# A fused Perceiver layer on one core: new prologue order and stage table, and the FFN's last product as two reduced-precision products

## The reference

```
x = x + xattn(layernorm(x), ctx, ctx)    # Q,K,V = proj(+bias); 16 heads of 16; softmax; @ Wh.T + bh
x = x + attn(layernorm(x))               # causal linear attention: exp features of normalised q, k
x = x + ffn(layernorm(x)), where
  gate = x @ (w_gate/127).T ; up = x @ (w_up/127).T        # 768 hidden, integer weights -127..127
  h    = silu(gate) * up
  out  = h @ (w_down/127).T                                # "down": 256x768 times 768x256 per batch
```

## Time and profile before

| | |
|---|---|
| median of 3 runs (lowest, highest) | 905.61 us (902.4, 907.89) |
| the profiled execution's own time | 904.62 us |
| its span | 902.9 us |
| TensorE matmul busy | 838.8 us, 93% |
| VectorE busy | 424.6 us, 47% |
| ScalarE busy | 531.7 us, 59% |
| mean granted TensorE clock | 0.992 |

### The profile page before, as it was taken

The page is one execution under the profiler, slowest core; times in us unless marked ns, Lnnn a source line. Parts: engine busy times, 40 slices in busy tenths (PEclk is TensorE's granted clock), DMA queues, the critical chain, the costliest instruction groups (busy, mean ns, idle before and its releaser), DMA issues.

```text
span 902.9 us, 20688 instructions
## 1 busy us (share of the span) xinstructions
PE 838.8 (93%) x8883; PEld 578.2 (64%) x8883; DVE 424.6 (47%) x752; ACT 531.7 (59%) x578; POOL 47.8 (5%) x76
## 2 busy tenths in 40 slices
PE   6699999999999999999999999999899999988876
PEld 5566666656566666766656667766566666657655
DVE  6533235454644446534654446444654444213753
ACT  2177887767476666656557666666557666750101
POOL 1033000000000000000000000000000000000100
PEclk9899999999999999999999999999999999999989
DMA  6777664466333433246433332355433322201000
GB/s 174 233 216 225 214 205 166 141 213 189 114 142 141 141 141 117 100 159 176 142 140 142 141 114 88 128 187 139 166 140 141 119 111 77 71 23 26 1 1 15
DMA packets 58737, 120.08 MB, mean 133 GB/s; under 512 B 21521, under 2 KB 29713, under 8 KB 55121
## 3 DMA queue, kind: packets, MB, share of 16 engines
q1 hardware_dynamic: 56848, 114.31, 37.4%
q0 software_dynamic: 1792, 4.40, 1.7%
HBM read 78.84 MB, written 37.75 MB: 129 GB/s over the span
## 4 chain that ended last, share of the span: by engine, by line
PE 72%; DVE 12%; issue 6%; DMA 3%; ACT 3%; DVEq 2%; POOL 1%; SPq 0%; POOLq 0%; ACTq 0%
PE ps_o L752 22%; PE ps_s L764 16%; PE ps_pa L557 9%; PE ps_pa L596 9%; PE ps_pa L722 2%; ACT probs L1036 2%; PE ps_pa L697 2%; DMA oscr<-y 2%; PE ps_pa L709 1%; PE ps_pa L688 1%; PE ps_pa L674 1%; DVE kparts L1075 1%; DMA y<-oscr 1%; DVE feat L1276 1%; DVE ctx_lo L1061 1%
## 5 line engine op out<-in xcount | busy, mean ns | idle before, releaser
L1036 ACT ACTIVATE probs<-ps_s 128x1024 f32<-128x1024 f32 x512 | 496.2, 1023 | 250.6 <-PE ps_s L764 243.7
L752 PE MATMUL ps_o<-probs,values 128*17 128x256 f32 x4096 | 252.9, 381 | 0.0
L764 PEld LDWEIGHTS ps_s<-qstack,kstack 64*128 64x128 f32 x2048 | 138.7, 185 | 105.3 <-ACT probs L1036 54.4
L764 PE MATMUL ps_s<-qstack,kstack 64*128 64x256 f32 x2048 | 193.3, 305 | 9.6 <-ACT probs L1036 7.5
L752 PEld LDWEIGHTS ps_o<-probs,values 128*17 128x17 f32 x4096 | 103.3, 97 | 96.9 <-issue 7.9
L1073 DVE TENSOR_SCALAR kparts<-ps_pa,b_heads 128x512 fp32r<-128x512 f32 x64 | 48.0, 750 | 105.0 <-PE ps_pa L557 105.0
L1090 DVE TENSOR_TENSOR values<-ps_pa,bv_pair 128x512 f32<-128x512 f32 x64 | 44.2, 690 | 105.1 <-PE ps_pa L596 104.9
L596 PE MATMUL ps_pa<-wv_hi,ctx_hi 128*128 128x256 f32 x256 | 77.6, 303 | 2.1 <-DVE wv_lo L1061 1.6
L596 PE MATMUL ps_pa<-wv_lo,ctx_hi 128*128 128x256 f32 x256 | 72.1, 282 | 0.0
L596 PE MATMUL ps_pa<-wv_hi,ctx_lo 128*128 128x256 f32 x256 | 71.9, 281 | 0.0
L557 PE MATMUL ps_pa<-ctx_hi,wk_hi 128*128 128x512 f32 x128 | 58.0, 453 | 4.3 <-DVE kparts L1075 2.2
(11 more groups left out here) (238 smaller groups left out, 797.5 us busy)
## 6 DMA issues: line engine op xcount, KB each, us to landing
kstack<-kscr SPq DMA_DIRECT2D x96, 512.0 KB, 5.2
kscr<-kparts SPq DMA_DIRECT2D x64, 512.0 KB, 2.7
ctx_raw<-ctxT SPq DMA_DIRECT2D x32, 512.0 KB, 6.7
qstack<-qscr SPq DMA_DIRECT2D x12, 256.0 KB, 3.9
qscr<-qparts SPq DMA_DIRECT2D x4, 512.0 KB, 3.2
xh<-x SPq DMA_DIRECT2D x4, 256.0 KB, 5.9
kstack<-kstack SPq DMA_DIRECT2D x2, 512.0 KB, 6.4
qstack<-ksample SPq DMA_DIRECT2D x4, 256.0 KB, 3.8
```

Of the source, the lines that this page charges most:

```text
L752: last = mm(ps_o[32 * j:32 * j + DH + 1, g * S:(g + 1) * S], values[par][:, i, head_of_step(g, j), :], prob[:, j * S:(j + 1) * S], start=b ...
L764: last = mm(ps_s[s % 2][:, j * S:(j + 1) * S], kstack[par][rows, u, i * P:(i + 1) * P], queries[rows, u, :], start=True, stop=True)
L1036: nc.scalar.activation(probs[n % AHEAD][:, :], ps_s[n % 2][:, :], ACT.Exp, scale=float(DH) ** -0.5).then_inc(fast["exp_done"], 1)
```

## The change

1. Prologue. TensorE's first matmul no longer waits for the value bias. The weights `wq` are turned by ACT and not by VectorE, and are loaded ahead of the value bias, as `wv` is. `split_ctx(0)` stands ahead of the bias copy. Head stages go round four half banks of `ps_s`. The sampled maximum is worked out directly behind `q`; the values and the keys of chunk 1 come after it: values pair 0 ahead of the first score, pair 1 and both key units of chunk 1 in slots 0, 1 and 4 of chunk 0, whose own value slots move to 5 and 8. SP issues the shift ahead of the load of context chunk 2.
2. Tables. `AT` and `HEAD_AT` have new steps (the FFN stages and `down` earlier, the head stages earlier, `ln1T` to `norm1` later). `kbd` is cut into `kbd0` and `kbd1`. SP writes a batch's queries ahead of a key half in chunk 6, and stacks and shifts them in chunk 7 behind a wait for the previous tail's `down`.
3. The down product. `wd_sb` becomes fp32r (integers up to 127, exact in it). `gate{k}` on VectorE makes `hid` and then cuts it into a high and a low part, four blocks' parts in the idle query stack, two in `x_parts` (so gates 4 and 5 wait for `gu5`). `down_part` is then two fp32r matmuls where one fp32 matmul was. The integer weights come into `qk` and `y` in two DMAs and are cast from there.

```diff
 VALUE_SLOTS = {3: 0, 5: 1}
 KEY_SLOTS = {9: 0, 13: 1}
+FIRST_KEYS = {1: 0, 4: 1}
+FIRST_VALUES = {5: 0, 8: 1}
+HEAD = ["ln0", "ln0T", "q", "kbd0", "max0", "max1", "kbd1", "max2", "max3", "maxT"]
+HEAD_FIRST = ["ln0", "ln0T", "q", "kbd0", "kbd1", "max0", "max1", "max2", "max3", "maxT"]
-AT = {"o": 1, "oT0": 3, "oT1": 4, "yT": 12, "wh": 13, "ln1T": 17, "qk0": 19, "ss0": 19, "qk1": 21, "ss1": 21, "v": 24,
-      "norm0": 24, "norm1": 25, "qkT0": 25, "qkT1": 28,
+AT = {"o": 1, "oT0": 3, "oT1": 4, "yT": 12, "wh": 13, "ln1T": 19, "qk0": 20, "ss0": 20, "qk1": 22, "ss1": 22, "v": 24,
+      "norm0": 26, "qkT0": 26, "norm1": 27, "qkT1": 28,
...
-      "A4": 64, "A5": 70, "pv2": 72, "A6": 74, "A7": 78, "pv3": 82, "o2T0": 84, "o2T1": 85, "y2T": 88, "wout": 89,
-      "ln2T": 94, "gu0": 96, "gate0": 98, "gu1": 99, "gate1": 100, "gu2": 101, "gate2": 104, "gu3": 105, "gate3": 108,
-      "gu4": 109, "gate4": 112, "gu5": 115, "gate5": 116, "down": 124}
+      "A4": 64, "A5": 70, "pv2": 72, "A6": 74, "A7": 78, "pv3": 80, "o2T0": 84, "o2T1": 86, "y2T": 88, "wout": 90,
+      "ln2T": 94, "gu0": 96, "gate0": 98, "gu1": 100, "gate1": 101, "gu2": 102, "gate2": 103, "gu3": 104, "gate3": 105,
+      "gu4": 106, "gu5": 110, "gate4": 110, "gate5": 111, "down": 112}
-HEAD_AT = {"ln0": 86, "ln0T": 104, "q": 108, "kbd": 110, "max0": 112, "max1": 116, "max2": 117, "max3": 120,
-           "maxT": 121}
+HEAD_AT = {"ln0": 86, "ln0T": 92, "q": 99, "kbd0": 106, "max0": 108, "kbd1": 110, "max1": 114, "max2": 115,
+           "max3": 116, "maxT": 118}
...
-         **{f"max{n}": "kbd" for n in range(4)}}
+         **{f"max{n}": f"kbd{n // 2}" for n in range(4)}}
...
+        wd_int = [qk[:, :, :].rearrange("p t c -> p (t c)").bitcast(INT32).rearrange("p (k n) -> p k n", n=D),
+                  y[:, :, :].bitcast(INT32)]
         x_parts = [sb("x_hi", [P, CI, S], FP32R)[:, :, :], sb("x_lo", [P, CI, S], FP32R)[:, :, :]]
+        def hid_part(of, k, part):
+
+            n = 2 * k + part
+            return qstacks[of][:, n, :] if n < HALF else x_parts[(n - HALF) // CI][:, n % CI, :]
...
+            if alone == "head":
+                k = c.bank(clock, name) % BANKS_HEAD
+                return ps_s[k // 2][:, k % 2 * 512:(k % 2 + 1) * 512]
...
+        def keys_bank(q, j):
+
+            return ps_a if (q, j) in ((0, 1), (1, 0), (1, 1), (2, 0)) else ps_p
+
+        def parts_of(c, clock):
+
+            return 0 if c is general else clock[1] % 2
...
+            sp.dma_start(wq_rows.rearrange("p (i n) -> p i n", i=CI), wr(wqT)).then_inc(wq_in, 16)
+            sp.dma_start(wstage[:, CI * D:2 * CI * D].rearrange("p (i n) -> p i n", i=CI), wr(wvT)).then_inc(wv_in, 16)
             for t in range(2):
                 sp.dma_start(bv_pair[:, t * H:(t + 1) * H, :].rearrange("p h d -> p (h d)"),
-                             bv.partition_broadcast(P)).then_inc(b_in, 16)
-            sp.dma_start(wq_rows.rearrange("p (i n) -> p i n", i=CI), wr(wqT)).then_inc(wq_in, 16)
-            sp.dma_start(wstage[:, CI * D:2 * CI * D].rearrange("p (i n) -> p i n", i=CI), wr(wvT)).then_inc(wv_in, 16)
+                             bv.partition_broadcast(P)).then_inc(bv_in, 16)
...
             stack_queries(fast, 0, qstacks[0])
+            shift_queries(fast, head_of(0), qstacks[0])
+            load_ctx(fast, NCH, 2)
             sp.wait_ge(hot_in, 16)
             sp.dma_start(kstack[1][SLOTS:P:APART, :, :].bitcast(FP32), kstack[0][SLOTS:P:APART, :, :].bitcast(FP32)
                          ).then_inc(hot_in, 16)
-            load_ctx(fast, NCH, 2)
-            shift_queries(fast, head_of(0), qstacks[0])
             write_keys(fast, 1, 1)
...
+                    if b + 1 < B and p == HEAD_AT["q"] // STEPS:
+                        write_queries(fast, head_of(b + 1))
+                    if b + 1 < B and p == HEAD_AT["maxT"] // STEPS:
+                        if b:
+                            sp.wait_ge(fast["product"], fast.at("product", tail_of(b - 1), "down"))
+                        stack_queries(fast, b + 1, qstacks[(b + 1) % 2])
+                        shift_queries(fast, head_of(b + 1), qstacks[(b + 1) % 2])
                     if q + 2 < B * NCH:
                         write_key_half(fast, q + 2, p % 2, 0)
-                    if b + 1 < B and p == HEAD_AT["q"] // STEPS:
-                        write_queries(fast, head_of(b + 1))
-                        stack_queries(fast, b + 1, qstacks[(b + 1) % 2])
-                    if b + 1 < B and p == HEAD_AT["maxT"] // STEPS:
-                        shift_queries(fast, head_of(b + 1), qstacks[(b + 1) % 2])
                     if q + 2 < B * NCH:
                         write_key_half(fast, q + 2, p % 2, 1)
                     if b and p == AT["down"] // STEPS:
...
-                if j:
+                if q == 1:
+                    pe.wait_ge(fast["k_out"], 2 + j)
+                elif q == 2:
+                    pe.wait_ge(*((fast["v_ready"], q * PAIRS) if j else (fast["k_out"], q * 2)))
+                elif q and j:
                     pe.wait_ge(fast["k_out"], q * 2 + 1)
...
-            def down_part(c, k, bank, clock=None):
-
-                if clock is not None:
-                    pe.wait_ge(c["operand"], c.at("operand", clock, f"gate{k}"))
+            def down_part(c, k, bank, clock):
+
+                pe.wait_ge(c["operand"], c.at("operand", clock, f"gate{k}"))
                 for t in range(ST):
-
-                    last = mm(bank[:, t * D:(t + 1) * D], hid[:, k, t * P:(t + 1) * P], wd_sb[:, k, :],
-                              start=k + t == 0, stop=k == HB - 1, skip_group_check=True)
+                    for part in range(2):
+
+                        last = mm(bank[:, t * D:(t + 1) * D], hid_part(parts_of(c, clock), k, part)[:, t * P:(t + 1) * P],
+                                  wd_sb[:, k, :], start=k + t + part == 0, stop=k + part == HB, skip_group_check=True)
                 return last
...
-                if s in VALUE_SLOTS and q + 1 < B * NCH:
-                    project_values(q + 1, VALUE_SLOTS[s])
+                value_slots = VALUE_SLOTS if q else FIRST_VALUES
+                if q == 0 and s == 0:
+                    project_values(0, 1)
+                if q == 0 and s in FIRST_KEYS:
+                    project_keys(1, FIRST_KEYS[s])
+                if s in value_slots and q + 1 < B * NCH:
+                    project_values(q + 1, value_slots[s])
...
-            pe.wait_ge(b_in, 64)
+            pe.wait_ge(b_in, 32)
             pe.wait_ge(setup_dve, 2)
-            mm(ps_a[:, 0:2 * CI], ident_heads, b_rows[:, :], start=True, stop=True).then_inc(b_turned, 1)
-            project_keys(0, 0)
-            products(fast, ["ln0T"], head_of(0))
-            project_keys(0, 1)
+            mm(ps_s[1][:, 512:512 + 2 * CI], ident_heads, b_rows[:, :], start=True, stop=True).then_inc(b_turned, 1)
+            warm(ps_s[1], 5)
+            for j in range(CI):
+                project_keys(0, j)
+            products(fast, ["ln0T"], head_of(0), "head")
+            pe.wait_ge(wq_turned, 1)
+            products(fast, ["q"], head_of(0), "head")
+            warm(ps_p, 10)
+            products(fast, ["max0", "max1", "max2", "max3", "maxT"], head_of(0), "head")
             pe.wait_ge(setup_dve, 3)
-            products(fast, ["q"], head_of(0))
-            warm(ps_s[1], 7)
-            pe.wait_ge(setup_dve, 4)
-            for pair in range(PAIRS):
-                project_values(0, pair)
-                products(fast, [f"max{2 * pair}", f"max{2 * pair + 1}"], head_of(0))
-            project_keys(1, 0)
-            products(fast, ["maxT"], head_of(0))
-            project_keys(1, 1)
-            warm(ps_s[1], 12)
+            project_values(0, 0)
+            warm(ps_a, 3)
...
-            pool.dma_start(wd_sb[:, :, :].bitcast(INT32), wr(wdT)).then_inc(i_in, 16)
+            for k, part in zip((0, HB - CI), wd_int):
+                n = part.shape[1]
+                pool.dma_start(part, wr(wdT)[:, k:k + n, :]).then_inc(i_in, 16)
...
+            act.wait_ge(wq_in, 16)
+            nc.scalar.activation(by_heads(wq_sb), by_dims(wq_rows), ACT.Copy).then_inc(wq_turned, 1)
...
+                    if heads and n == 0:
                         dve.wait_ge(c["q_shift"], heads * 16)
-                    for j in range(CI):
-                        last = v.tensor_tensor(ksample[:, j, :, :],
-                                               kparts[:, 0, j, 0:SAMPLE].bitcast(FP32).unsqueeze(1).to_broadcast([P, H // 2, SAMPLE]),
-                                               head_mask[:, :].unsqueeze(2).to_broadcast([P, H // 2, SAMPLE]), ALU.mult)
+                    last = v.tensor_tensor(ksample[:, n, :, :],
+                                           kparts[:, 0, n, 0:SAMPLE].bitcast(FP32).unsqueeze(1).to_broadcast([P, H // 2, SAMPLE]),
+                                           head_mask[:, :].unsqueeze(2).to_broadcast([P, H // 2, SAMPLE]), ALU.mult)
...
```

(56 more changed lines are left out.)

47 lines of the change are left out of this document (23 added, 24 removed).

## The result

The changed kernel takes 911.5 us (median of 7 runs, 907.85 to 917.49), the kernel before, on the same chip, 905.5 (7 runs, 902.4 to 911.35). The ratio is 1.007, 95% interval 1.0042 to 1.0098: slower, by more than the 0.5% of a no-change. The forecast was 902.5, range 894.5 to 908, with 0.07 on slower. The profiled execution after is the fastest of its seven: own time 907.85, span 906.0. Its span is 3.1 us longer than that of before; the medians lie 6 apart.

What follows compares the result with a forecast made beforehand. TensorE was taken to bound the loop, with chains of engines in the prologue and last tail. The terms summed to -3.1 us, 904.62 to 901.5; with the median 1.0 higher, 902.5, range 894.5 to 908.

Steps and rivals of the forecast that it cites:

- First score: Prologue: the first score comes at 32.5 instead of 41.66, -9.2 us.
- Low clock behind the first score: Start of chunk 0: low clock lasts until 36, so 3.5 us behind the first score lose half, +1.5 us.
- Rival B: Chunk 0's first quads: TensorE stays at 1.2 GHz, deciding from a low clock until 42; up to 910 us, chance 0.12.
- the three units and batch 0's waits: Three units moved into chunk 0 cost +4.8 us; shorter waits at batch 1's first score and `max0` save 2.1.
- Added waits (a) to (d): In the loop, in order: `qkT0` 2.5, paired products 0.32, `down` 1.65, `max1` 0.9; +5.5, +1.3, +3.3, +1.8 us.
- 2.0 at `gu4`: Batch 3's last two chunks: 2.0 us idle at `gu3` and `gu4`, without a unit between, until ACT passes an exp.
- Rival A: Loop: the added waits at `qkT0`, `down` and `max1`, 10.6 us, don't come; 892 us, chance 0.32.
- Last two chunks of batch 3: From 763.5, the last value product ends at 810.4 instead of 811.1, -0.7 us.
- Down product: Batches 1 and 2: 24 fp32r matmuls take 2.85 us instead of 5.37, saving 2.5 each, -5.1 us.
- Rival C: Down product: weight loads don't overlap matmuls, so its 5.1 us saving is gone; 907.6 us, chance 0.02.
- Last tail: Serial end behind the loop: longer gates and `gu5` ahead of gates 4 and 5 put output at 900.75, +2.9 us.
- the signs that I had named for a wrong prediction: No waits at `qkT0` and `down`, or chunk 0 longer than 24 us by a stall before chunk 1's first score.

Runs made afterwards that it cites:

- the wait filled: The changed kernel with nine dummy matmuls issued on TensorE in the wait of `qkT0`, its late place kept: 907.6 us, ratio 1.0025 to the kernel before.
- the three groups: The follow-up kernels' runs, each group on one chip beside the kernel before, which took 905.1 to 906.0 us in them; the changed kernel did not run again.

## Why the prediction was wrong

Step by step, measured in the profiled executions, in which the change was forecast at -3.1 and came out at +3.1 of span:

- **First score** -9.2: came at 29.30, not 32.5, so -12.4. This term was mis-sized by the landing of the first context chunk. The earlier trace rows has three loads with 3.8, 4.2 and 6.8; I took the longest for the first. It was there by 5.5, and the cut ended at 7.5 for 10.1. This error went in the change's favour and hid a part of the others.
- **Low clock behind the first score** +1.5: the clock was 0.50 until 30.6, 1.3 us past the first score, and most of that lies before a wait for the exp. About half a microsecond. But this is one draw. In two other profiles with the same prologue (the wait filled, fp32 down in the changed kernel) it was low until 38.2 and 38.4, and `yT` of batch 1 came 2.2 and 2.8 us later. Rival B's 42 was not reached, a part of it was. With the three units and batch 0's waits the prologue and batch 0 were forecast at -5.0 and gave -8.9 at `yT` of batch 1.
- **Added waits (a) to (d)**: right in place and size (2.46 for 2.5, 0.29 to 0.34 for 0.32, 1.65 for 1.65, 0.78 for 0.9; 1.74 for 2.0 at `gu4` of batch 3). Rival A had no part in it.
- **What was missing in them**: the low clock. This is the step that failed. I priced an idle stretch of TensorE at its own length. In the terms of the prediction, (a), (c) and the 2.0 at `gu4` are waits without a term for what comes behind them. I had looked for low clock only in the prologue, because the loop of before runs at full clock with single waits of up to 1.76 (at `yT` of batch 2), and took that for a rule. Four falls in the profiled loop cost 1.7 each, 6.7 together.
- **`ln0T`** at step 92: its product waits 1.03 and 1.05 for the layernorm behind `wout`, which sits in the one bank. I had given this stage no row: 2.1.
- **Last two chunks of batch 3** -0.7: from the quad with `gu0` to the first transposes of the tail it took 50.6 (760.77 to 811.32) for 49.0 (763.46 to 812.45), so +1.6. 1.7 of that is the low stretch behind `gu4`, counted above.
- **Down product** -5.1: 24 matmuls took 2.9 as forecast. As for its worth, the runs with fp32 show that it was a loss of 3 us in the changed kernel, and is a gain of 3 in the loop only with `down` started gate by gate. Rival C fell: loads and matmuls lay in 0.118 us each.
- **Last tail** +2.9: the stretch from the end of the loop to the output took 89.4 for 85.4, so +4.0. The FFN part is 3.9, with low clock under `down`; I had 2.9. `qkT1` with its wait of 1.57 adds 1.4, which I hadn't seen, and the other parts gave 1.3 back.

-3.2 -1.0 +6.7 +2.1 +1.1 is 5.7 of the 6.3 between forecast and profile. Neither of the signs that I had named for a wrong prediction came: the waits at `qkT0` and `down` are there, and chunk 0 took 23.7 us. Both signs tested where waits lie, and none what a wait costs.

The medians lie another 3 us apart, which no profile shows. The clock of all runs can be compared instead. The 63 runs of the kernel before in the three groups have a median granted clock of 0.986, the 7 of the changed kernel 0.973. Within the runs of the kernel before, the 13 with a clock of 0.989 or more have a median of 903.6 us and the 9 with 0.981 or less one of 908.4: 0.5 us per thousandth. At that slope 13 thousandths are 6.5 us, and my estimate for the changed kernel at the clock of before is 905. The slope is a correlation between runs of one kernel; that it carries over to another is not shown.

The Trainium skill ("TensorE: Matmul & The Clock Gate", section "HAM oscillation — how this bites in real kernels") tells of a matmul loop with a wait in each turn, which meets the throttled clock again in every turn and pays half of the throttled time. The trace agrees on the pattern and the price: three batches, the same wait, the same stretch behind it, 1.7 of 3.4 us. It differs in the wait: the page's come from DMAs and are longer than the 2.46 here, which comes from one operation of another engine too many.

What is not settled: which wait is followed by a fall and which isn't. In the loops (40 to 812 us) of the fourteen profiles there are 34 falls, counted as behind a wait when they begin in it or within 1.6 us of its end. They came behind 14 of the 15 waits of 2.4 us or more (the fifteenth is the 2.47 of batch 1 in the changed kernel with fp32 down), behind 8 of the 25 between 1.6 and 2.0, and behind 8 of 98 between 0.95 and 1.5, these eight all at `feat0` with 1.10. The last four came behind a pair of waits for the exp, 0.9 and 0.4. Runs of one kernel differ in their mean clock, so a single profile shows one draw.

## What to carry to other kernels

In a loop that TensorE fills, price an idle stretch at its length plus the low clock that can follow it: 1.7 us, here nearly always behind 2.46, in about one case of three behind 1.65 to 1.99, and seldom behind 1.10. Look at the mean granted clock over many runs of each kernel, not at one profile, before you compare times. A wait that cannot go can be filled with dummy matmuls. A cheaper operation on the bounding engine whose operands need more work on another one is worth its arithmetic only where that work has cover; measure it in the loop and in the serial tail apart, and let each part start on its own operand. In a table with one bank and one strict queue, a stage moved by one step to save a wait can make two others.
